# A four-layer graph network on one core: the attention passes' edge one-hots built on ScalarE, and the first pass's messages as four products with a per-partition scalar

## The chip, the cores and the metric

One NeuronCore of a Trainium2 chip runs the whole program. The metric is the time of one launch on the device, in microseconds (us). Engine names are those of the profile: PE (TensorE, matmuls), DVE (VectorE), ACT (ScalarE), POOL (GpSimd), SP (SyncE, which issues DMAs).

## What is computed

The input is a graph of 3,125 nodes with 128 features and 53,125 edges, sorted by target node. Four layers follow each other, each added to `x` after a layer norm with Relu. Cut to what matters:

```python
h = relu(layernorm(x)); x = x + gat(h)            # softmax over each target's edges, one head
h = relu(layernorm(x)); x = x + relational(h)     # sum of proj[src, type] into dst
h = relu(layernorm(x)); x = x + two_gcn_layers(h)
h = relu(layernorm(x)); x = x + two_transformer_convs(h)   # softmax attention, four heads

# an attention layer, for the edges e: src -> dst
alpha = score(q[dst], k[src]);  p = exp(alpha - segment_max(alpha, dst)[dst])
out   = segment_sum(v[src] * p, dst) / segment_sum(p, dst)
```

So there are three attention passes over the edges (the GAT layer, called the first pass, and the two transformer convolutions, called the second and third) and three linear passes (one relational, two GCN).

## The kernel before

**Tiles.** The 53,125 edges are padded to 13 chunks of 8 groups of 4 tiles of 128 edges: 104 groups, 416 tiles. One edge lies on one partition. Since edges are sorted by target, the targets of a tile lie in a window of 128 nodes, and those of a group in a span of 512.

**A pass of attention.** POOL issues for every tile one indirect DMA (line 465) that gathers the source rows of its 128 edges into a ring in SBUF (24 slots of one group in the first pass, 15 in the others); for a group beyond the ring it first waits for `msg_ready` of the group that had the slot. PE brings the target rows to the edges with a one-hot (node by edge) that ACT makes in `targets` (a Square, line 628, and a Relu, line 630). DVE makes the scores: in the second and third pass by a product for each group (`products`, which waits for the gather) and a reduction (`head_sums`), in the first pass once for each chunk (`scores`, which waits for all eight gathers of the chunk). A chain through DVE, PE and ACT once for each chunk gives the maxima and exponentials.

**The part that is changed.** DVE's `messages(s)` (line 880) does two things for group s, both as a tensor_tensor on 128 x 512 elements in float32 through the helper `tt` (line 716): the value rows times the factor of the edge (into `msg`, which signals `msg_ready`), and the one-hot by edge, `iota_j == dstP` with both inputs broadcast (into `Sb`, 3 slots, which signals `s_ready`). PE's `node_sums(s)` (line 1300) waits for `s_ready`, clears a PSUM bank `NU[s % 2]` and multiplies messages by one-hots into it, then does the same with the factors into `MTB`. DVE's `add_sums(s)` adds both to the sums in SBUF (`numS`, `extS`). DVE runs `messages(s - 11)` in its step s and `add_sums(s - 13)` before it in the same step, so `s_ready` and `msg_ready` of a group tell PE as well that the bank of two groups earlier has been read. PE runs `expand(s + 1)` and then `node_sums(s - 12)` in its step s.

**The order of ACT.** In each step s of its `attention` (line 618) ACT does `edge_terms(s)` (in the second and third pass it waits for DVE's product of group s and copies 16 columns, line 639), `targets(s + 4)`, and once in a chunk `exponentials(c)`, which waits for the maxima.

**A linear pass** gathers in the same way (line 479); DVE makes its one-hots with the same tensor_tensor, and has no messages to make.

## Time and profile before

| | us |
|---|---|
| median of three runs (3841.62, 3859.76, 3859.91) | 3859.76 |
| the profiled execution, its time | 3848.41 |
| the profiled execution, its span | 3846.6 |
| POOL busy in the span | 2596.3 (67%) |
| PE busy | 2344.7 (61%) |
| DVE busy | 1864.5 (48%) |
| ACT busy | 587.7 (15%) |
| mean granted TensorE clock | 0.706 |

Some 1.8 us lie around the span. How to read it: the busy shares are means over six passes with different limits. The gathers of the six passes run, by the span's clock, from 90 to 685 (first attention), 806 to 1327, 1387 to 1907 and 1943 to 2463 (linear), 2537 to 3104 and 3191 to 3768 us (second and third attention). Between and behind them lie stages without gathers: the end of an attention pass takes some 40 us after its last gather, and then tables are built. The page gives the chain of work that ended last, the groups of instructions, and the waits; a gap of 0.30 us before each gather is put down to "issue".

### The profile page before, as it was taken

Reading aid. Unit: us, or ns where it says so; the run is one execution under the profiler, and the core shown is the slowest. Engines: PE = TensorE matmul, PEld = TensorE weight load, DVE = VectorE, ACT = ScalarE, POOL = GpSimd, SP = SyncE. Lnnn points to the kernel's source line nnn. Section 1 sums busy time; section 2 is a strip of 40 time slices with the busy share of each in tenths; the row PEclk is TensorE's granted clock in tenths of the full one; section 3 lists DMA queues with packets and bytes.
Section 4 is the critical chain, followed back from the end, with each engine's and each line's share of the span. In section 5 each row is a group of like instructions: output and inputs, shape, how many; then the busy total and the mean of one; then the engine's idle time right before and its main releaser. Section 6 shows DMA issues by size and latency. Waiting matters only on the chain.

```text
span 3846.6 us, 42630 instructions
## 1 busy us (share of the span) xinstructions
PE 2344.7 (61%) x12256; PEld 1786.2 (46%) x12460; DVE 1864.5 (48%) x3957; ACT 587.7 (15%) x1289; POOL 2596.3 (67%) x2561
## 2 busy tenths in 40 slices
PE   4477777664444554444454444457777785777776
PEld 2465555333333343333333333336566654656665
DVE  4365555633322332222232222337777784777777
ACT  2322221220000020000000000132222202222220
POOL 1777777047777647777667777447777736777773
PEclk9988888865555565555555555568888896888888
DMA  4433333131222112212122221156666616656651
GB/s 93 87 73 74 73 72 63 66 110 53 53 53 53 43 47 53 53 53 53 45 58 53 53 53 53 41 167 171 167 170 176 170 57 184 170 164 167 169 162 36
DMA packets 345045, 356.63 MB, mean 93 GB/s; under 512 B 125614, under 2 KB 267637, under 8 KB 344821
## 3 DMA queue, kind: packets, MB, share of 16 engines
q0 software_dynamic: 93184, 219.12, 21.4%
q1 hardware_dynamic: 245494, 132.86, 13.1%
q10 hardware_dynamic: 6148, 1.93, 0.3%
q8 instruction: 114, 1.87, 0.2%
q14 instruction: 105, 0.86, 0.1%
HBM read 323.81 MB, written 30.05 MB: 92 GB/s over the span
## 4 chain that ended last, share of the span: by engine, by line
POOL 64%; issue 20%; PE 7%; DVE 4%; DMA 3%; ACT 1%; ACTq 1%; DVEq 0%; SPq 0%; POOLq 0%
POOL gathered_rows L465 33%; POOL gathered_rows L479 31%; PE QX L1157 4%; DMA gathered_rows<-key_value_rows,src_index 2%; PE NU L1157 1%; PE MTB L1157 1%; DVE messages L716 1%; ACTq L531 0%; DVE x_rows L716 0%; DVE query_key_products L716 0%; PE MID L1190 0%; DVE extra_sums_transposed L716 0%; PE MTB L1190 0%; ACT h_transposed L592 0%; DMA gcn_columns<-in_L_gnn_be_dram 0%
## 5 line engine op out<-in xcount | busy, mean ns | idle before, releaser
L1157 PE MATMUL NU<-gathered_rows 128*128 128x128 f32 x2496 | 636.8, 437 | 809.6 <-DMA gathered_rows<-gcn_rows,src_index 540.5
L465 POOL DMA_INDIRECT gathered_rows<-key_value_rows,src_index x832 | 889.1, 1069 | 312.0 <-issue 251.3
L479 POOL DMA_INDIRECT gathered_rows<-gcn_rows,src_index x832 | 785.8, 944 | 346.8 <-issue 252.9
L1157 PEld LDWEIGHTS NU<-gathered_rows 128*128 128x128 f32 x2496 | 554.5, 327 | 992.3 <-issue 977.1
L716 DVE TENSOR_TENSOR sums_transposed<-sums_transposed,NU 128x512 f32 x624 | 425.5, 682 | 1163.1 <-PE NU L1157 1160.4
L465 POOL DMA_INDIRECT gathered_rows<-gat_rows,src_index x416 | 467.8, 1125 | 207.5 <-issue 126.5
L479 POOL DMA_INDIRECT gathered_rows<-relation_rows,src_relation_index x416 | 393.9, 947 | 147.8 <-issue 126.5
L1157 PEld LDWEIGHTS NU<-edge_node_onehot,messages 128*128 128x128 f32 x2496 | 382.4, 219 | 17.7
L1157 PE MATMUL NU<-edge_node_onehot,messages 128*128 128x128 f32 x2496 | 379.0, 302 | 11.2 <-issue 3.0
L1157 PE MATMUL MTB<-edge_node_onehot,edge_factors 128*8 128x128 f32 (+1 forms) x2496 | 343.1, 283 | 0.0
L1157 PE MATMUL QX<-query_window,node_edge_onehot 128*128 128x132 f32 (+1 forms) x1248 | 201.6, 304 | 146.4 <-DMA query_window<-query_rows 81.1
L716 DVE TENSOR_TENSOR query_key_products<-QX,gathered_rows 128x512 f32<-128x512 f32 x208 | 142.1, 683 | 292.4 <-DMA gathered_rows<-key_value_rows,src_index 257.1
L628 ACT ACTIVATE window_distance<-dst_in_window_row,minus_partition 128x512 bf16<-128x512 bf16 x312 | 225.1, 721 | 336.9 <-PE QX L1157 279.1
L1157 PEld LDWEIGHTS MTB<-edge_node_onehot,edge_factors 128*8 128x8 f32 (+1 forms) x2496 | 232.8, 93 | 90.0 <-issue 11.2
L1157 PEld LDWEIGHTS QX<-query_window,node_edge_onehot 128*128 128x128 f32 x1248 | 176.4, 217 | 174.4 <-issue 161.2
L1157 PE MATMUL NU<-start_penalty,zero_weights 128*128 128x512 bf16 x420 | 239.5, 570 | 9.6 <-DVE edge_node_onehot L716 9.3
L716 DVE TENSOR_TENSOR extra_sums_transposed<-extra_sums_transposed,MTB 8x512 f32 (+1 forms) x312 | 209.3, 671 | 43.8 <-PE MTB L1157 43.4
L716 DVE TENSOR_TENSOR gathered_rows<-iota_window,dst_in_window_by_edge 128x512 f32<-128x512 f32 x312 | 212.6, 685 | 5.7 <-DMA relation_rows<-gathered_rows 5.7
L716 DVE TENSOR_TENSOR edge_node_onehot<-iota_window,dst_in_window_by_edge 128x512 f32<-128x512 f32 x312 | 211.2, 677 | 0.0
L716 DVE TENSOR_TENSOR messages<-gathered_rows,edge_factors 128x512 f32<-128x512 f32 x312 | 211.0, 676 | 0.0
L1157 PE MATMUL QX<-query_window,relation_weights 128*128 128x132 f32 x832 | 162.2, 356 | 77.3 <-DMA query_window<-query_rows 40.3
L1157 PEld LDWEIGHTS QX<-query_window,relation_weights 128*128 128x128 f32 x832 | 140.1, 252 | 100.1 <-issue 90.2
(255 smaller groups left out, 2206.7 us busy)
## 6 DMA issues: line engine op xcount, KB each, us to landing
query_window<-query_rows SPq DMA_DIRECT2D x832, 66.0 KB
dst_in_window_row<-dst_in_window SPq DMA_DIRECT2D x156, 256.0 KB, 3.5
gathered_rows<-gcn_rows,src_index POOLq DMA_INDIRECT x832, 2.5
gathered_rows<-key_value_rows,src_index POOLq DMA_INDIRECT x832
relation_rows<-gathered_rows SPq DMA_DIRECT2D x25, 512.0 KB, 2.6
gathered_rows<-gat_rows,src_index POOLq DMA_INDIRECT x416, 2.6
query_window<-gat_target_scores SPq DMA_DIRECT2D x416, 2.0 KB
gathered_rows<-relation_rows,src_relation_index POOLq DMA_INDIRECT x416, 2.5
```

What stands on the lines that cost most here:

```text
L465: pool.indirect_dma_start(out=rows_of(a, s)[:, t, :], out_offset=None, in_=a["table"], in_offset=bass.IndirectOffsetOnAxis(ap=srcI[:, TPG ...
L479: pool.indirect_dma_start(out=lrows[:, TPG * (K % LRING) + t, :], out_offset=None, in_=p["table"], in_offset=bass.IndirectOffsetOnAxis(ap= ...
L628: own.step(act.activation(STa[:, s % 2, :], drow_sb[:, half, q:q + TPG * P], ACT.Square, bias=neg_iota_p[:]))
L716: return dve.tensor_tensor(o, x, y, op)
L1157: return pe.matmul(o, l, r, start=start, stop=stop)
```

## The change

ACT takes over the one-hots by edge in all three attention passes. A new function `edge_onehots(s)` makes the four tiles of a group with four Square activations of 128 x 128 (`(dst - iota)^2`, the bias being the column of `dstP`), waits for its own last one, and turns them into ones and zeros with a Relu of `1 - x` over 128 x 512, in place. It is called at the end of ACT's step for group s - 10, two groups ahead of PE's use, and waits until PE has done with the slot, three groups earlier (`ex_ready`). ACT's loop runs 7 steps longer so that the last groups are covered. DVE no longer makes them. PE's `node_sums` waits for `msg_ready` as well as `s_ready`. In the first pass, which has one head, the messages of a group are no longer one tensor_tensor but four tensor_scalar products of 128 x 128 with the tile's factor as a per-partition scalar.

```diff
@@ scalar engine, attention
+                def edge_onehots(s):
+
+                    to = Sb[:, s % SBN]
+                    if s == 0 and k == 0:
+                        act.wait_ge(S["idx_ready"], 2)
+                    if s >= SBN:
+                        act.wait_ge(S["ex_ready"], b + s - SBN + 1)
+                    for t in range(TPG):
+                        last = act.activation(to[:, t, :], iota_j[:], ACT.Square,
+                                              bias=dstP[:, TPG * s + t:TPG * s + t + 1], scale=-1.0)
+                    own.step(last)
+                    act.wait_ge(own.sem, own.value())
+                    act.activation(to, to, ACT.Relu, bias=1.0, scale=-1.0).then_inc(S["s_ready"], 1)
+
                 for s in range(TS):
                     targets(s)
-                for s in range(NG + 3):
+                for s in range(NG + LAG - 2):
                     if s < NG:
                         edge_terms(s)
                     if s + TS < NG:
...
                     if r == 2 and 0 <= c < NCH:
                         exponentials(c)
+                    if 0 <= s + 2 - LAG < NG:
+                        edge_onehots(s + 2 - LAG)
@@ vector engine, messages(s)
-                    tt(msg[:, s % 2].rearrange("p t (h d) -> p t h d", h=H), v, f, ALU.mult).then_inc(S["msg_ready"], 1)
-                    tt(Sb[:, s % SBN], iota_j[:].unsqueeze(1).broadcast_to([P, TPG, P]),
-                       dstP[:, TPG * s:TPG * s + TPG].unsqueeze(2).broadcast_to([P, TPG, P]),
-                       ALU.is_equal).then_inc(S["s_ready"], 1)
+                    if L3:
+                        last = tt(msg[:, s % 2].rearrange("p t (h d) -> p t h d", h=H), v, f, ALU.mult)
+                    else:
+                        for t in range(TPG):
+                            last = dve.tensor_scalar(msg[:, s % 2, t, :], v[:, t, 0, :],
+                                                     pe8[:, s // GPC % 2, 0, TPG * g + t:TPG * g + t + 1], None, ALU.mult)
+                    last.then_inc(S["msg_ready"], 1)
@@ tensor engine, node_sums(s)
                     pe.wait_ge(S["s_ready"], sb0 + s + 1)
+                    pe.wait_ge(S["msg_ready"], b + s + 1)
                     clear(NU[s % 2], P)
```

## Rows read from the trace of the kernel before

**Rows 1.** The page's chain that ended last, by line.

```profile
POOL gathered_rows L465 33%; POOL gathered_rows L479 31%; PE QX L1157 4%; DMA gathered_rows<-key_value_rows,src_index 2%; PE NU L1157 1%; PE MTB L1157 1%; DVE messages L716 1%; ACTq L531 0%; DVE x_rows L716 0%; DVE query_key_products L716 0%; PE MID L1190 0%; DVE extra_sums_transposed L716 0%; PE MTB L1190 0%; ACT h_transposed L592 0%; DMA gcn_columns<-in_L_gnn_be_dram 0%
```

**Rows 2.** By stretch: length; busy PE, PEld, DVE, ACT, POOL; clock; DMA share, GB/s.

```profile
90.00:685.00 595.00, 405.70 (x2654) 321.62 (x2700) 310.24 (x689) 144.67 (x245) 467.82 (x416) 0.85 0.36 73
...
1387.00:1907.00 520.00, 252.30 (x922) 187.46 (x939) 137.65 (x214) 0.00 (x0) 393.12 (x416) 0.51 0.20 53
...
2537.00:3104.00 567.00, 406.87 (x2598) 332.54 (x2645) 403.58 (x813) 153.25 (x348) 439.56 (x416) 0.85 0.61 171
3104.00:3144.00 40.00, 33.87 (x248) 25.30 (x251) 36.51 (x74) 0.71 (x4) 0.00 (x0) 0.97 0.02 4
3191.00:3768.00 577.00, 413.22 (x2602) 333.87 (x2649) 403.99 (x813) 151.87 (x347) 449.55 (x416) 0.84 0.60 168
```

**Rows 3.** POOL's groups by form: busy, mean ns, idle before and releasers.

```profile
L479 POOL DMA_INDIRECT gathered_rows<-gcn_rows,src_index x832 | 785.8, 944 | 346.8 <-issue 252.9 <-DMA gcn_rows<-gathered_rows 93.9
L465 POOL DMA_INDIRECT gathered_rows<-gat_rows,src_index x416 | 467.8, 1125 | 207.5 <-issue 126.5 <-DMA gat_target_scores<-gathered_rows 81.1
```

**Rows 4.** Waits: POOL on messages, whole span; DVE on gathers, 2537 to 3104.

```profile
POOL gathered_rows L465 <- DVE messages L716: 7.6, 25, 0.3
...
DVE query_key_products L716 <- DMA gathered_rows<-key_value_rows,src_index: 122.8, 50, 4.7
```

**Rows 5.** Timeline of POOL and of DVE, 2616.8 to 2620, second attention pass.

```profile
2618.09 1.42 POOL L465 DMA_INDIRECT gathered_rows<-key_value_rows,src_index  x1 [0.30 <-issue]
...
2617.41 0.68 DVE L716 TENSOR_TENSOR messages<-gathered_rows,edge_factors 128x512 f32<-128x512 f32 x1
2618.01 0.69 DVE L716 TENSOR_TENSOR edge_node_onehot<-iota_window,dst_in_window_by_edge 128x512 f32<-128x512 f32 x1
```

**Rows 6.** Timeline of POOL and of DVE, 1100 to 1101.4, a linear pass.

```profile
1100.17 0.94 POOL L479 DMA_INDIRECT gathered_rows<-relation_rows,src_relation_index  x1 [0.30 <-issue]
...
1100.58 0.68 DVE L716 TENSOR_TENSOR gathered_rows<-iota_window,dst_in_window_by_edge 128x512 f32<-128x512 f32 x1
```

**Rows 7.** Timeline of the first pass: a burst, and DVE's wait ahead of a chunk.

```profile
437.75 1.73 POOL L465 DMA_INDIRECT gathered_rows<-gat_rows,src_index  x1 [0.30 <-issue]
...
436.78 0.68 DVE L716 TENSOR_TENSOR extra_sums_transposed<-extra_sums_transposed,MTB 3x512 f32 x1 [0.49 <-PE MTB L1157]
...
437.99 0.67 DVE L716 TENSOR_TENSOR edge_node_onehot<-iota_window,dst_in_window_by_edge 128x512 f32<-128x512 f32 x1
438.90 0.69 DVE L716 TENSOR_TENSOR sums_transposed<-sums_transposed,NU 128x512 f32 x1 [0.24 <-PE NU L1157]
440.08 0.68 DVE L716 TENSOR_TENSOR extra_sums_transposed<-extra_sums_transposed,MTB 3x512 f32 x1 [0.48 <-PE MTB L1157]
...
410.05 0.21 DVE L716 TENSOR_TENSOR query_edge_term<-gathered_rows,QX 128x32 f32<-128x32 f32 x1 [12.96 <-DMA gathered_rows<-gat_rows,src_index]
```

**Rows 8.** Timeline, 514.6 to 515.7: a gather and a small tensor_scalar that started in it.

```profile
514.65 0.95 POOL L465 DMA_INDIRECT gathered_rows<-gat_rows,src_index  x1 [0.30 <-issue]
...
515.18 0.46 DVE L946 TENSOR_SCALAR max_change_by_feature<-max_change,chunk_continues 1x128 f32<-1x128 f32 x1
```

**Rows 9.** Timeline at 31 us: eight tensor_scalar products of 128 x 128, no gather about.

```profile
31.12 1.65 DVE L742 TENSOR_SCALAR relation_weights<-query_key_products,relation_coefficients 128x128 f32<-128x128 f32 x8
```

**Rows 10.** ACT's groups by form: busy, mean ns, idle before and releasers.

```profile
L628 ACT ACTIVATE window_distance<-dst_in_window_row,minus_partition 128x512 bf16<-128x512 bf16 x312 | 225.1, 721 | 336.9 <-PE QX L1157 279.1 <-DMA dst_in_window_row<-dst_in_window 57.8
L630 ACT ACTIVATE node_edge_onehot<-window_distance 128x512 f32<-128x512 bf16 x156 | 98.2, 630 | 5.0
L586 ACT ACTIVATE normed_block<-x_rows,minus_mean_scaled,inverse_deviation 128x128 f32<-128x128 f32 x100 | 48.9, 492 | 14.7 <-DVE minus_mean_scaled L770 14.2 <-PE MTB L1190 0.2
L639 ACT COPY query_edge_term<-QX 128x16 f32<-128x16 f32 x208 | 38.8, 187 | 832.2 <-DVE query_key_products L716 825.6 <-PE QX L1157 6.5
...
L686 ACT ACTIVATE h_transposed<-sums_transposed,gcn_small 128x512 f32<-128x512 f32 x12 | 9.1, 802 | 1.4 <-DVE gcn_small L1107 1.4
```

**Rows 11.** Busy time in the end of the second pass, 3126 to 3141 (columns of Rows 2).

```profile
3126.00:3141.00 15.00, 14.24 (x110) 10.94 (x111) 15.00 (x26) 0.00 (x0) 0.00 (x0) 1.00 0.00 1
```

## The prediction

> **What bounds the kernel now.** I read the chain that ended last first, then busy time by stretch, then POOL's groups and waits, then the timeline of POOL beside that of DVE. The chain lies on POOL's gathers: 33% of the span at line 465 (attention), 31% at line 479 (linear) [rows 1]; before each gather lies a gap of 0.30 us [rows 5, 6]. Busy time by stretch says how much of each pass is POOL itself. A linear pass is 416 gathers, 393.1 us busy in 520: 0.945 us each, and with the gap 1.25 us, so 416 x 1.25 = 520 is the whole pass [rows 2, 3]. The attention passes have the same 416 gathers and the same gap (126.5 us for the first pass's 416 is 0.304 each), but are busy 467.8, 439.6 and 449.6 us [rows 2, 3]. The difference to 393.1 is 74.7, 46.5 and 56.5 us, 177.7 together, and it explains their 595, 567 and 577 us to a few tenths. So POOL never stands still in a pass; its gathers are stretched. It doesn't wait for its ring: the only wait on messages is 25 gaps of at most 0.3 us, no longer than the usual gap [rows 4]. DVE waits for gathers, not the reverse (122.8 us of the second pass) [rows 4]. **The prize is those 177.7 us**, plus what the ends of passes give.
>
> **What stretches a gather.** Lay the timelines side by side. In the second pass a gather starts at 2618.09, while DVE is in messages and one-hot, 2617.41 to 2618.70; it takes 1.42 us instead of 0.95 and ends at 2619.51, 0.82 after the one-hot's end [rows 5]. In the first pass a gather of 1.73 us (437.75 to 439.48) again ends 0.82 after the one-hot's end at 438.66 [rows 7]. So a gather that starts while DVE holds a pair of SBUF inputs waits for the end of the train and then needs 0.82 us; it loses what was left of the train less 0.12. In a linear pass a one-hot of 0.68 us that starts 0.41 us into the gather stretches nothing: 0.94 us [rows 6]. It has ended when the next gather begins; DVE's other two-input work there is of the same size, and the pass has no stretch at all [rows 2]. With the phase left to chance, a train of length T costs on average (T - 0.12)^2 / (2 x 1.25) for each group. For messages and one-hot, T = 2618.70 - 2617.41 = 1.29: 0.55 us, times 104 groups 57 us a pass; measured 74.7, 46.5, 56.5. The rule has the right size.
>
> **Part 1: the one-hots leave DVE in the second and third pass.** The train shrinks to the messages alone, 0.68 us [rows 5]: 0.56^2 / 2.5 = 0.125 us a group, 13 us a pass. Small two-input operations of the chunk's chain stay; for them I add 2 us and take 15 us of stretch a pass. Gain: 46.5 + 56.5 - 30 = **73 us**. Bounds: if the stretch only went down in proportion to the train (0.68/1.29 of 103 is 54) the gain is 49; if it vanished as in the linear passes, 103.
>
> **Part 2: what ACT takes.** For each group four Squares of 128 x 128 and a Relu of 128 x 512. No row shows that Square. From above: 0.49, the activation of the same size with two per-partition operands; from below, the 0.72 of the 512-column Square with one, less 384 columns at (0.80 - 0.49) / 384 us, the slope between the two sizes with two: 0.41 [rows 10]. The Relu goes by the 0.63 of line 630. So 2.2 to 2.6 us a group. With line 628, line 630 and the copy of line 639 (0.72 + 0.63 + 0.19) ACT's step is 3.8 to 4.2 us [rows 10] against the 5.0 us in which POOL now delivers a group at best. It is hidden, under POOL's gathers; by how much, 0.8 to 1.2 us. PE uses the one-hot two of its steps later, and ACT's wait for the slot is on PE work of three groups earlier, so both waits have a step or more in hand. Queued behind ACT's new wait are the next copy (for PE's expand), the next `targets` (four groups ahead) and once a chunk the exponentials, which DVE awaits; a delay of 2 us there falls within a chunk of 40 us in which DVE still waits for gathers. I cost it at nothing. PE's added wait for `msg_ready` is fulfilled 0.6 us earlier than the one-hot was: nothing. In the first pass's bursts PE and DVE do a group in 3.3 us (436.78 to 440.08) [rows 7]; ACT without the copy needs 3.6 to 4.0, which can make a burst of 8 up to 5 us longer, covered by the 13 us that DVE idles before each chunk [rows 7].
>
> **Part 3: the first pass's messages.** Eight tensor_scalar of this shape take 1.65 us [rows 9], with 0.28 for the last: 0.196 apart, so four make 3 x 0.196 + 0.28 = 0.87 us against 1.29 for the train before. If they only acted on a gather's start, the rule gives 0.75^2 / 2.5 = 0.225, 23 us for the pass. But a one-source operation meets the gather at its end too: the small tensor_scalar that starts at 515.18, 0.53 us into a gather, takes 0.46 instead of 0.27 and ends 0.04 after the gather does [rows 8]. If the four start in the last 0.45 us of a gather they are pushed to its end, run to 0.91 behind it, and the next gather, 0.30 behind, loses 0.91 - 0.30 + 0.82 - 0.945 = 0.48 us. Averaged over the phases that is 0.36 x 0.48 + 0.24 x 0.6 = 0.32 a group, 33 us. If, beyond that, they keep a gather in progress from finishing, another 0.4 us in 0.4 of the phases, 17 us, comes to it, 50. The first pass measures 1.3 times my rule (74.7 to 57), so from 23 to 62, I take 42. Gain: 74.7 - 42 = **33 us** (13 to 52). The Trainium skill has a rule for this, in "SBUF — State Buffer", section "Who interferes with whom": two SBUF inputs contend with GpSimd's reads, while tensor_scalar in its two-port mode shuts GpSimd out altogether, so that it can't write descriptors. The case of rows 8 points that way (they collide at the gather's end), and by that rule the first pass would keep its stretch.
>
> **Part 4: the ends.** After the last gather the second pass takes 40 us [rows 2]. In its middle both engines are full: PE 14.24 and DVE 15.00 of 15 us at full clock, 2.4 us a group [rows 11]. Taking 0.6 us off DVE doesn't help where PE needs the same 2.4. Only the chain of the last chunk, which DVE sets, gains: I take 1 us for each of three ends, **3 us**, between -3 (exponentials queued behind one-hots) and 7 (12 groups x 0.6) for each.
>
> **The sum.** 73 + 33 + 3 = 109 us off the profiled execution's 3848.4 (span 3846.6 and 1.8 around it): 3739. The median of the runs is 11 us above the profiled one, which would give 3751; I say 3745, between them.
>
> **Rivals.** *A: the products take back what they save in the first pass.* The push and the lockout together leave its stretch at 75 us: 3848 - 73 - 3 = 3772, 3784 by the median; 3778. For: rows 8. Against: the train is shorter by a third. It is also the time by the Trainium skill's rule above. *B: the passes aren't POOL's for long.* PE is busy 407 of 567 us in the second pass at a mean clock of 0.85 [rows 2], 3.9 us a group, and its chain waits come on top; with POOL at 5.05 us a group it may set the pace at 5.2, 0.15 x 208 = 31 us less gain: 3776. For: PE's share goes to 77% and more; against: DVE's 122.8 us of waiting for gathers would first have to be used up. *C: no stretch is left in passes 2 and 3*, as in the linear ones, and 23 in the first: 3853 - 103 - 52 - 3 = 3695. *D, slower: the four products take turns with gathers.* If each tensor_scalar is held to the end of a gather, as the one in rows 8, a group's messages take 4 x 1.25 = 5.0 us instead of 0.8. DVE's group is then 5.0 + 1.2 = 6.2, and a chunk 8 x 6.2 plus 7 for its chain (46 now, less 13 idle, less 8 x 3.3) = 57 us against 595 / 13 = 46 now; 11 x 13 chunks = 143 us, less 73: 70 slower, 3923. It decides from the point where a group's messages exceed about 3.5 us: the 1.2 of today, 0.7 idle in the burst (0.24 + 0.48) and 13/8 = 1.6 idle ahead of the chunk [rows 7]. Against: products queued back to back should go as a train, as messages and one-hot do now. *E: the change doesn't do what it says*, since ACT becomes the pace: it would need more than 5.0 us a group, and 5.7 to be slower than today, where I find at most 4.2; then 3850, no change.
>
> **Chances and range.** Forecast 0.64, A 0.13, B 0.10, C 0.05, D 0.04, E 0.04. The likeliest case alone spans 3845 less the gains' bounds, which are hardly all met at once: 3715 to 3780. The range of 8 in 10 takes in A, B and half of the way to C: 3702 to 3800. About 0.5% is what a measurement of this kernel can tell from no change, 19 us: faster 0.91, same 0.04, slower 0.05.
>
> **What would show it.** Right: gathers of line 465 at a mean near 0.98 us in passes 2 and 3 and 1.04 in the first, with the gap still 0.30; DVE busy down by some 190 us, ACT up by some 700 and still below 85% in any pass; no idle of PE before its sums put down to ACT. A shows as a first pass still at 1.1 us a gather; B as gaps above 0.30 before gathers, ended by messages; D as tensor_scalar products far above 0.28 us; E as PE's sums waiting for the one-hots. The prediction is wrong if POOL stands still for anything but its 0.30 us, or if single trains of 0.68 us hit gathers more often than by chance.

## The result, and the profile after

The changed kernel takes **3722.64 us**, the median of 4 runs (3713.34 to 3726.67), against 3856.38 for the kernel before (4 runs, 3841.62 to 3859.91): a ratio of 0.9658, 95% interval 0.9642 to 0.9674. The forecast was 3745, in a range of 3702 to 3800. The profiled execution took 3726.67 us (span 3724.8), 121.7 us less than the 3848.41 of before.

From the page of the changed kernel: busy time of each engine; the chain that ended last, by engine; the two groups of attention gathers; the two new groups on ScalarE (columns: busy us, mean ns | idle before and what ended it).

```profile
PE 2389.6 (64%) x12460; PEld 1788.2 (48%) x12460; DVE 1711.9 (46%) x3957; ACT 1147.3 (31%) x2849; POOL 2460.8 (66%) x2561
...
POOL 57%; issue 19%; PE 13%; DVE 5%; DMA 3%; ACT 1%; ACTq 1%; SPq 1%; DVEq 0%; POOLq 0%
...
L465 POOL DMA_INDIRECT gathered_rows<-key_value_rows,src_index x832 | 816.6, 982 | 318.3 <-issue 252.8
...
L465 POOL DMA_INDIRECT gathered_rows<-gat_rows,src_index x416 | 403.9, 971 | 209.4 <-issue 124.7
...
L659 ACT ACTIVATE edge_node_onehot<-iota_window,dst_in_window_by_edge 128x128 f32<-128x128 f32 x1248 | 394.6, 386 | 27.3 <-PE MTB L1176 25.1
...
L663 ACT ACTIVATE edge_node_onehot<-edge_node_onehot 128x512 f32<-128x512 f32 x312 | 196.5, 630 | 9.9
```

The chain still lies on POOL. From here on, **stretch** is the busy time of a pass's 416 gathers less the 393.1 us that they take in an undisturbed linear pass [rows 2]. It is read off the two groups: 403.9 - 393.1 = 10.8 us in the first pass (before 74.7 [rows 3]), and 816.6 - 786.2 = 30.4 in the second and third together (before 46.5 + 56.5 = 103). Line 465's share of the chain is 25%, before 33% [rows 1].

By stretch of time, the three attention passes of the changed kernel (length; busy PE, PEld, DVE, ACT, POOL; clock; DMA share, GB/s):

```profile
92.00:623.00 531.00, 423.88 (x2700) 329.75 (x2700) 277.22 (x875) 315.86 (x725) 403.93 (x416) 0.86 0.41 82
2483.00:3018.00 535.00, 403.89 (x2650) 325.92 (x2651) 351.80 (x720) 319.74 (x813) 407.79 (x416) 0.86 0.66 181
...
3110.00:3645.00 535.00, 403.96 (x2650) 326.91 (x2651) 351.62 (x720) 318.65 (x812) 408.40 (x416) 0.86 0.66 181
```

They answer to 595, 567 and 577 us [rows 2]: 64, 32 and 42 less. That is the stretch and nothing else: 531 is 416 gathers of 0.971 us and their gaps of 0.305. What lies outside the passes gained nothing: the stages between them and the tail add up to 565 us in this profile, 551 before, and 550 in a second profile of the changed kernel, so the 14 us more of this one are most likely scatter between executions and not a cost of the change.

The messages on VectorE, from its groups by form, and two moments of the first pass, POOL beside VectorE (start, duration):

```profile
L732 DVE TENSOR_TENSOR messages<-gathered_rows,edge_factors 128x512 f32<-128x512 f32 x208 | 140.9, 677 | 0.0
L904 DVE TENSOR_SCALAR messages<-gathered_rows,edge_factors 128x128 f32<-128x128 f32 x416 | 95.5, 291 | 0.0
```

```profile
244.47 1.07 DVE L904 TENSOR_SCALAR messages<-gathered_rows,edge_factors 128x128 f32<-128x128 f32 x4
244.56 0.94 POOL L465 DMA_INDIRECT gathered_rows<-gat_rows,src_index  x1 [0.30 <-issue]
...
277.32 1.29 POOL L465 DMA_INDIRECT gathered_rows<-gat_rows,src_index  x1 [0.30 <-issue]
277.63 1.01 DVE L904 TENSOR_SCALAR messages<-gathered_rows,edge_factors 128x128 f32<-128x128 f32 x4
278.91 0.94 POOL L465 DMA_INDIRECT gathered_rows<-gat_rows,src_index  x1 [0.30 <-issue]
```

At 244.5 a gather starts 0.09 us into the four products and takes its plain 0.94; it is the products that pay, 1.07 us against 0.86 where no gather runs beside them. At 277.3 the products begin 0.31 us after the gather and it takes 1.29. Over the first pass, the 54 gathers that start in the 0.6 us after the first product's start lose 0.05 us on average, the 34 that start in the 0.6 us ahead of it 0.18 (each by its own length less 0.945).

### The profile page after: what moved, and what is told of

Its sections match the earlier page's. It is cut to its first block, busy times and chain, and to the rows that moved or that the text cites. A ratio compares the mean times of both kernels' runs of the same rounds, so it can differ in the third digit from the quotient of the medians.

```text
span 3724.8 us, 44708 instructions
## 1 busy us (share of the span) xinstructions
PE 2389.6 (64%) x12460; PEld 1788.2 (48%) x12460; DVE 1711.9 (46%) x3957; ACT 1147.3 (31%) x2849; POOL 2460.8 (66%) x2561
## 4 chain that ended last, share of the span: by engine, by line
POOL 57%; issue 19%; PE 13%; DVE 5%; DMA 3%; ACT 1%; ACTq 1%; SPq 1%; DVEq 0%; POOLq 0%
POOL gathered_rows L479 32%; POOL gathered_rows L465 25%; PE QX L1176 6%; PE NU L1176 3%; PE MTB L1176 3%; DMA gathered_rows<-key_value_rows,src_index 2%; DVE messages L732 1%; ACTq L531 1%; DMA query_window<-gat_target_scores 0%; PE MID L1176 0%; DMA open_tiles<-end_ahead_penalty 0%; DVE query_key_products L732 0%; DVE x_rows L732 0%; PE MID L1209 0%; PE MTB L1209 0%
## 5 line engine op out<-in xcount | busy, mean ns | idle before, releaser
L465 POOL DMA_INDIRECT gathered_rows<-key_value_rows,src_index x832 | 816.6, 982 | 318.3 <-issue 252.8
L465 POOL DMA_INDIRECT gathered_rows<-gat_rows,src_index x416 | 403.9, 971 | 209.4 <-issue 124.7
L659 ACT ACTIVATE edge_node_onehot<-iota_window,dst_in_window_by_edge 128x128 f32<-128x128 f32 x1248 | 394.6, 386 | 27.3 <-PE MTB L1176 25.1
L1176 PE MATMUL MTB<-edge_node_onehot,edge_factors 128*8 128x128 f32 (+1 forms) x2496 | 358.7, 292 | 0.0
L1176 PE MATMUL NU<-start_penalty,zero_weights 128*128 128x512 bf16 x624 | 329.5, 528 | 10.4 <-DVE messages L732 9.9
L663 ACT ACTIVATE edge_node_onehot<-edge_node_onehot 128x512 f32<-128x512 f32 x312 | 196.5, 630 | 9.9
```

The lines of the kernel that those rows point to most:

```text
L465: pool.indirect_dma_start(out=rows_of(a, s)[:, t, :], out_offset=None, in_=a["table"], in_offset=bass.IndirectOffsetOnAxis(ap=srcI[:, TPG ...
L659: last = act.activation(to[:, t, :], iota_j[:], ACT.Square, bias=dstP[:, TPG * s + t:TPG * s + t + 1], scale=-1.0)
L663: act.activation(to, to, ACT.Relu, bias=1.0, scale=-1.0).then_inc(S["s_ready"], 1)
L1176: return pe.matmul(o, l, r, start=start, stop=stop)
```

## Experiments

My theory going in was that of the prediction: VectorE's operations with two SBUF inputs hold a gather that starts among them, and what is gained is the shorter train of such work. The rivals: the length of VectorE's chain or of its instructions counts, not their inputs; short instructions let a gather in between; the products with a per-partition scalar, not the one-hots, bring the gain; ScalarE has no room. Every edit is against the changed kernel, unless it says otherwise. The first four kernels ran on another chip than all the rest and are told last. A gather's **loss** is its own length less 0.945 us.

### The changed kernel again

> The changed kernel once more, beside the kernel before on the same chip. In the first group of runs the kernel before itself took 4493 us, 16% more than the 3856 it took where the change was measured, and its linear passes took 588 us and not 520, with gaps of 2 to 8 us before gathers; so this run says which of the two conditions holds here. My theory: where linear passes take 520 us, the ratio is 0.966 as before, with 11, 15 and 16 us of stretch over 0.945 us a gather in the three attention passes. Rival (the gaps of the first group are a property of that chip and hit every kernel alike): linear passes of 588 us, the same small stretch, but a ratio within 0.5% of 1.01, because gaps and not the stretch set the passes there.

3716.98 us (3707.84 to 3722.22) beside 3850.09 for the kernel before: 0.9655 (0.9627 to 0.9684). Stretch 11.4, 12.0 and 19.0 us, linear passes 520 us. This is the base for the next three.

### One-hots alone

```diff
-                    if L3:
-                        last = tt(msg[:, s % 2].rearrange("p t (h d) -> p t h d", h=H), v, f, ALU.mult)
-                    else:
-                        for t in range(TPG):
-                            last = dve.tensor_scalar(...)
+                    last = tt(msg[:, s % 2].rearrange("p t (h d) -> p t h d", h=H), v, f, ALU.mult)
```

> One-hots on ScalarE in all three attention passes, the first pass's messages as one product over the group as before the change. In the first group of runs this kernel's stretch was 17, 19 and 17 us. My theory (a train of 0.68 us of two-input work costs a gather little, the pair of messages and one-hot much): the same 15 to 20 us in each pass, so the one-hots bring nearly all of the gain also in the first pass, and where linear passes take 520 us the time is within 10 us of the changed kernel: ratio 0.966 to 0.969. Rival (the four products are what saved the first pass): its stretch stays at 40 or more and the time is 25 us or more above the changed kernel, ratio 0.973 or more.

3744.18 us (3739.89 to 3762.29), ratio 0.9737 (0.9699 to 0.9774), 27 us above the changed kernel. Its two groups of gathers, and a moment of its first pass:

```profile
L465 POOL DMA_INDIRECT gathered_rows<-key_value_rows,src_index x832 | 824.6, 991 | 311.1 <-issue 254.3
...
L465 POOL DMA_INDIRECT gathered_rows<-gat_rows,src_index x416 | 432.4, 1039 | 207.0 <-issue 126.4
```

```profile
260.45 0.68 DVE L732 TENSOR_TENSOR extra_sums_transposed<-extra_sums_transposed,MTB 3x512 f32 x1 [0.49 <-PE MTB L1171]
260.82 1.73 POOL L465 DMA_INDIRECT gathered_rows<-gat_rows,src_index  x1 [0.30 <-issue]
261.06 0.67 DVE L732 TENSOR_TENSOR messages<-gathered_rows,edge_factors 128x512 f32<-128x512 f32 x1
```

My expectation fell, and the rival's numbers came in. The second and third pass are as in the changed kernel (38.4 us together), but the first keeps 432.4 - 393.1 = 39.3 us. So **both parts count in the first pass**: the one-hots take it from 74.7 to 39.3, the products from 39.3 to 11. The moment shows why one two-input message of 0.67 us costs more there than I had it: the gather had started 0.24 us *before* the messages, and is held all the same, to 0.82 us after their end (261.73 + 0.82 = 262.55). Most starts up to 0.45 us ahead are caught in this pass; 29 gathers that began 0.15 to 0.45 us ahead of the messages lost 0.73 on average.

Of the pass's 39.3 us, 27 are lost by gathers that start in the 0.6 us ahead of the messages, and 9 by those that start during them. Widening the prediction's rule by 0.45 us gives (0.56 + 0.45)^2 / 2.5 = 0.41 us a group, 42 us a pass, near the 39.3; but for the train of before it gives 109 where 74.7 were measured, so it is no rule either. In the second pass 20 gathers in the same position lost only 0.16. What VectorE does just before the messages goes with it: in eight profiles in which linear passes take 520 us, of the gathers that start 0.15 to 0.45 us ahead of two-input work, all 60 lost more than 0.4 us where `extra_sums_transposed` came before that work, none of 78 where `max_after_tile` did, and 68 of 258 where `query_key_products` did. Why is not shown.

### The one-hots stay on VectorE, cut in four, one input each (edit of the kernel before)

```diff
-                    tt(Sb[:, s % SBN], iota_j[:].unsqueeze(1).broadcast_to([P, TPG, P]),
-                       dstP[:, TPG * s:TPG * s + TPG].unsqueeze(2).broadcast_to([P, TPG, P]),
-                       ALU.is_equal).then_inc(S["s_ready"], 1)
+                    for t in range(TPG):
+                        last = dve.tensor_scalar(Sb[:, s % SBN, t, :], iota_j[:], dstP[:, TPG * s + t:TPG * s + t + 1], None, ALU.is_equal)
+                    last.then_inc(S["s_ready"], 1)
```

> The kernel before with only this edit: the one-hot by edge stays on VectorE in all three attention passes but is made by four tensor_scalar of 128 x 128 (is_equal with a per-partition scalar) and not by one operation with two SBUF inputs over 128 x 512. Messages stay as they were. My theory (short instructions hand the port over between them, so that a gather gets in after at most one of them): the train is as long as before, 0.68 + 4 x 0.2, but the stretch falls from 75, 46 and 56 us to 20 to 35 in each pass; the time falls by 75 to 110 us, ratio 0.971 to 0.981, without any work moved to ScalarE. Rival 1 (length of the train is what counts, whatever it is cut into): stretch as in the kernel before, ratio 0.99 to 1.00. Rival 2 (the two-port mode of tensor_scalar shuts GpSimd out for the whole train): stretch above the kernel before, ratio above 1.00.

3772.91 us (3763.96 to 3778.35), ratio 0.9796 (0.9769 to 0.9822).

```profile
L465 POOL DMA_INDIRECT gathered_rows<-key_value_rows,src_index x832 | 833.7, 1002 | 311.2 <-issue 253.0
...
L465 POOL DMA_INDIRECT gathered_rows<-gat_rows,src_index x416 | 439.6, 1057 | 207.9 <-issue 125.9
...
L886 DVE TENSOR_SCALAR edge_node_onehot<-iota_window,dst_in_window_by_edge 128x128 f32<-128x128 f32 x1248 | 283.9, 284 | 0.0
```

The train of messages and one-hots is longer than before the change, 1.49 us against 1.27, yet the stretch is 46.5 us in the first pass and 47.5 in the other two together, 7 and 9 more than with the one-hots on ScalarE. The time and the two later passes came in as expected (22.7 and 24.7 us); the first pass's 46.5 lies above my 20 to 35. Both rivals fall. **Most of what moving the one-hots to ScalarE brings is to be had on VectorE**, by giving them one SBUF input: 84 of 100 us of stretch (178 to 94, against 178 to 78), and 77 of 106 us of time. This doesn't say yet whether it is the single input or the shortness of the four.

### The messages of passes two and three cut in four, two inputs as before

```diff
-                        last = tt(msg[:, s % 2].rearrange("p t (h d) -> p t h d", h=H), v, f, ALU.mult)
+                        for t in range(TPG):
+                            last = tt(msg[:, s % 2, t, :].rearrange("p (h d) -> p h d", h=H), v[:, t], f[:, t], ALU.mult)
```

> The changed kernel, and in the second and third pass the messages too are made by four operations of 128 x 128, with two SBUF inputs as they were. My theory (it is the length of one instruction that a gather waits out): the 15 and 16 us of stretch fall to 3 to 10 each, and the time is 8 to 20 us under the changed kernel, ratio to it 0.995 to 0.998. Rival (two-input instructions back to back hold on as one train, now 0.8 us long): 20 to 25 us of stretch each, 8 to 15 us slower than the changed kernel.

3711.68 us (3706.09 to 3713.57), ratio 0.9638 (0.9617 to 0.9659): 5 us under the changed kernel, which the two intervals don't tell apart. Gathers of the two passes, and two moments of the second:

```profile
L465 POOL DMA_INDIRECT gathered_rows<-key_value_rows,src_index x832 | 814.7, 979 | 311.1 <-issue 255.7
```

```profile
2608.55 1.72 POOL L465 DMA_INDIRECT gathered_rows<-key_value_rows,src_index  x1 [0.30 <-issue]
2608.56 0.88 DVE L732 TENSOR_TENSOR messages<-gathered_rows,edge_factors 128x128 f32<-128x128 f32 x4
...
2627.47 0.99 POOL L465 DMA_INDIRECT gathered_rows<-key_value_rows,src_index  x1 [0.30 <-issue]
2627.36 0.88 DVE L732 TENSOR_TENSOR messages<-gathered_rows,edge_factors 128x128 f32<-128x128 f32 x4
```

814.7 - 786.2 = 28.5 us of stretch against 31.1 in the run beside it. Neither my 6 to 20 nor the rival's 40 to 50. The moments show that both happen. The first gather isn't let in between the four: it ends 0.83 us after the last of them (2609.44), just as with one long operation. The second starts 0.11 us into the four and is let in: it ends 0.22 us after the last of them, which is 0.82 after the first.

Of the 94 gathers that start early enough in the four to be held to their end, 56 were, 27 ended 0.82 us after the first, second or third, and 11 lost nothing; of the 79 that start so in the single operation of the run beside it, 78 were held to its end. The four together last 0.88 us and not 0.67, for which the rule asks 34 us from those 94; being let in halves it to 17.5, so the sum stays where it was (20.8 in the run beside it). **Shortness helps some gathers, but with two inputs it gained nothing that can be told from scatter**, so it is not what brought the 84 us of the run before. What decides whether a gather is let in isn't shown.

### One more VectorE operation for each group: one input, then two

To settle inputs against length, two kernels add behind each group's messages an operation whose result nobody uses. In both it waits for its own predecessor (left out here), and is written here with `spare` for the unused tile.

```diff
                     last.then_inc(S["msg_ready"], 1)
...
+                    dve.tensor_reduce(spare, iota_j[:].unsqueeze(1).broadcast_to([P, TPG, P]), AX.X, ALU.add)...
```

> The changed kernel, and behind each group's messages VectorE makes one more operation whose result nobody uses: a tensor_reduce of 128 x 512 with ONE SBUF input. Each of its instructions is as long as a two-input product. On the other chip this kernel's stretch stayed at 6 to 9 us a pass. My theory (only the second SBUF input holds a gather's reads, the length of an instruction doesn't matter): the stretch stays at 10 to 20 us in each of the three attention passes. VectorE gets 0.67 us more for a group, some 70 us a pass, beside gathers that still set the pace; only the ends of passes and the chunk's chain pay: 0 to 25 us over the changed kernel in all. Rival (any long VectorE instruction between a gather's start and its reads holds it): 30 us or more of stretch a pass, as for messages and one-hot before the change, 60 to 120 us over the changed kernel.

```profile
L466 POOL DMA_INDIRECT gathered_rows<-key_value_rows,src_index x832 | 816.8, 982 | 313.9 <-issue 254.8
...
L466 POOL DMA_INDIRECT gathered_rows<-gat_rows,src_index x416 | 403.3, 969 | 206.5 <-issue 124.0
...
L912 DVE TENSOR_REDUCE normed_block<-iota_window 128x4 f32<-128x512 f32 x312 | 209.3, 671 | 0.0
```

3723.41 us (3717.82 to 3729.78), ratio 0.9672 (0.9643 to 0.97): 312 operations of 671 ns cost nothing that can be measured, and the stretch is that of the changed kernel to a few tenths (10.2 and 30.6 us).

```diff
                     last.then_inc(S["msg_ready"], 1)
...
+                    tt(spare, iota_j[:].unsqueeze(1).broadcast_to([P, TPG, P]),
+                       dstP[:, TPG * s:TPG * s + TPG].unsqueeze(2).broadcast_to([P, TPG, P]), ALU.is_equal)...
```

> The changed kernel, and behind each group's messages VectorE makes again the comparison with TWO SBUF inputs that the change took away (same operands, result to a spare tile, nobody waits for it). Nothing else goes back: ScalarE still makes the one-hots in use. My theory: the stretch comes back, 40 to 65 us in passes two and three, 30 to 60 in the first (its four products are one-input, so the train there is shorter than before the change), together 110 to 170 of the 178 before; time 70 to 125 us over the changed kernel. Rival (the gain came from a shorter VectorE chain, or from who produces the one-hots, not from the port): the same as with the added reduction, whose instructions are as long.

```profile
L466 POOL DMA_INDIRECT gathered_rows<-key_value_rows,src_index x832 | 893.9, 1074 | 311.0 <-issue 251.1
...
L466 POOL DMA_INDIRECT gathered_rows<-gat_rows,src_index x416 | 446.7, 1074 | 208.2 <-issue 124.7
...
L734 DVE TENSOR_TENSOR normed_block<-iota_window,dst_in_window_by_edge 128x512 bf16<-128x512 f32 x312 | 211.3, 677 | 0.0
```

3834.91 us (10 runs, 3826.13 to 3847.92), ratio 0.9961 (0.9943 to 0.998). As many operations, 677 ns against 671, and the stretch is 53.6 + 107.7 = 161 us, of the 178 before the change. ScalarE still makes the one-hots in use; **the comparison costs 111 us more than the reduction of the same length** (3834.91 less 3723.41), more than 80% of the change's gain. This pair of runs carries the explanation.

The two operations differ in one more thing than their inputs: the comparison writes 512 columns, the reduction 4. The changed kernel's own trace settles that. VectorE's additions of the node sums write 512 columns and are as long, but one of their two inputs, `NU`, lies in PSUM:

```profile
L732 DVE TENSOR_TENSOR sums_transposed<-sums_transposed,NU 128x512 f32 x624 | 426.6, 684 | 1237.2 <-PE NU L1176 1236.2
```

In its three attention passes 140 gathers start during one of them with no messages about; the average loss is 0.00 us, the largest 0.01. So neither length nor the columns written hold a gather; a second input in SBUF does.

### No message with two SBUF inputs at all

```diff
                     if L3:
-                        last = tt(msg[:, s % 2].rearrange("p t (h d) -> p t h d", h=H), v, f, ALU.mult)
+                        for t in range(TPG):
+                            for h in range(H):
+                                last = dve.tensor_scalar(msg[:, s % 2, t, HD * h:HD * h + HD], v[:, t, h, :],
+                                                         pe8[:, s // GPC % 2, h, TPG * g + t:TPG * g + t + 1], None, ALU.mult)
```

> The changed kernel, and in the second and third pass the messages are sixteen tensor_scalar of 128 x 32 for a group (one for each tile and head, factor per partition), so that no product of messages has two SBUF inputs in any pass. My theory (two SBUF inputs are what a gather waits for; four short two-input products saved nothing, 28.5 us of stretch against 31): 12 to 19 us of stretch in passes two and three fall to 3 to 8 each. VectorE pays for it: sixteen at 0.07 to 0.13 us against 0.68, 0.4 to 1.4 us more a group, free within a pass as long as its group stays below 5.0 us, paid at the three ends of passes with 12 groups each: time -15 to +25 us against the changed kernel. Rival (it is a train of VectorE instructions on the port that counts, one input or two): the train is now 1.2 to 2 us long and the stretch goes up to 40 us or more in each of the two passes.

```profile
L465 POOL DMA_INDIRECT gathered_rows<-key_value_rows,src_index x832 | 791.8, 952 | 374.1 <-issue 230.1
...
L903 DVE TENSOR_SCALAR messages<-gathered_rows,edge_factors 128x32 f32<-128x32 f32 x3328 | 518.4, 246 | 0.0
```

Its second pass (timeline), its waits of POOL (us in total, times, longest), and the pass by stretch:

```profile
2603.61 2.68 DVE L903 TENSOR_SCALAR messages<-gathered_rows,edge_factors 128x32 f32<-128x32 f32 x16
2604.07 0.95 POOL L465 DMA_INDIRECT gathered_rows<-key_value_rows,src_index  x1 [0.30 <-issue]
...
POOL gathered_rows L465 <- DVE messages L903: 84.8, 94, 3.0
...
2476.00:3027.00 551.00, 392.90 (x2595) 311.60 (x2596) 496.18 (x2058) 316.70 (x801) 395.73 (x416) 0.88 0.63 176
```

3786.65 us (3785.7 to 3789.95), ratio 0.9836 (0.9811 to 0.9861). The theory of the two inputs holds at its sharpest: a train of 2.68 us leaves the gather in it at 0.95, and the two passes' stretch falls to 791.8 - 786.2 = 5.6 us. But **the price was mis-sized**, and the time is 70 us above the changed kernel where I expected -15 to +25: a product of a quarter of the columns takes 246 ns against 291, so sixteen take 518.4 / 208 = 2.49 us a group and not 1.1 to 2.1. VectorE is busy 496 of 551 us, and gathers now wait for it. These waits for messages are 28 us a pass over the usual gaps, and the stretches of time behind the two passes grow by 20 us each (110 and 101 us against 90 and 80). 25 us of stretch gained, some 95 lost.

### How much cover ScalarE has

```diff
+                    for again in range(2):
+                        for t in range(TPG):
+                            last = act.activation(spare[:, t, :], iota_j[:], ACT.Square,
+                                                  bias=dstP[:, TPG * s + t:TPG * s + t + 1], scale=-1.0)
+                        ...
                     for t in range(TPG):
                         last = act.activation(to[:, t, :], iota_j[:], ACT.Square,
```

> The changed kernel, and before each group's four Squares ScalarE makes eight more of the same kind into a spare tile (2 x 1.28 us a group). My theory (ScalarE's step of 3.1 to 3.5 us is hidden under the 5.0 us in which GpSimd delivers a group, with 1.5 to 1.9 us of cover): 5.7 to 6.1 us a group exceed the cover, gathers get gaps ended by messages, and each attention pass lasts 590 to 635 us instead of 533; in all 170 to 300 us over the changed kernel. Rival (VectorE and PE wait for ScalarE anyway, so there is no cover now): all 2.56 x 104 = 266 us a pass are paid, some 800 us over it.

By stretch: the first pass and the stage behind it, the second pass, and the stage behind that.

```profile
91.00:628.00 537.00, 412.00 (x2363) 318.18 (x2364) 244.91 (x777) 465.98 (x1273) 403.23 (x416) 0.82 0.39 79
628.00:827.00 199.00, 149.72 (x737) 90.86 (x735) 97.44 (x339) 150.60 (x391) 3.37 (x2) 0.90 0.19 72
2559.00:3130.00 571.00, 386.19 (x2586) 313.49 (x2586) 347.08 (x711) 523.78 (x1514) 419.67 (x416) 0.89 0.62 170
3130.00:3244.00 114.00, 84.29 (x475) 57.60 (x475) 69.85 (x176) 67.42 (x216) 20.78 (x17) 0.90 0.15 46
```

3924.49 us (3919.05 to 3931.14), ratio 1.02 (1.0171 to 1.0229), 207 us over the changed kernel. That is within the 170 to 300 expected, but not where I put it: I expected 590 to 635 us for each pass, and they last 536, 570 and 570. The first pass lasts only 5 us longer, since its ring of 24 groups lets the gathers run on while ScalarE falls behind; the bill comes after it, 199 us instead of 121. Pass and stage together cost 83, 63 and 55 us more, 0.8, 0.6 and 0.5 us for each of 104 groups. The eight Squares add 2.48 us a group in the trace (from the first Square to the end of the Relu, 4.40 us against 1.92), so 1.7 to 1.95 us of it were covered. That is the room which the change's own one-hots left, if anything too small a figure: the gathers of the second and third pass are also stretched more here, 54.8 us against 31.0, which is 24 of the 207 us.

### The same four questions on another chip

The first four kernels ran on a chip where the kernel before itself took 4492.87 us (19 runs, 4464.72 to 4507.96).

> The one-hots by edge on ACT in all three attention passes, but the first pass's messages left as one tensor_tensor of 128 x 512. Port theory (a gather is stretched by what is left of one two-input DVE instruction, and can slip in between short ones): passes 2 and 3 as in the changed kernel, stretch 14 to 16 us each; in the first pass a single instruction of 0.68 us instead of four of 0.27, stretch 13 to 20 us instead of 10.8; time 3725 to 3735, a little above the changed kernel's 3722. Rival (what counts is DVE's time): DVE has 0.2 us less for each group of the first pass, so 3705 to 3722, below it.

> The kernel before with only the first pass's messages as four tensor_scalar products; all one-hots stay on DVE. Port theory: gathers slip in between the products and only the one-hot's 0.68 us stays as a block, so the first pass's stretch falls from 74.7 us to 25 to 40, passes 2 and 3 keep their 103: 3805 to 3825. Rival (DVE's time): DVE has 0.2 us more for each group of the first pass, nothing is gained: 3856 to 3870. If the products shut POOL out as a block of 0.87 us that grows the train to 1.5 us: first pass slower by 10 to 25 us, 3865 to 3880.

> The changed kernel with a reduction of 128 x 512 to 128 x 4 added on DVE behind the messages of every group, about 0.67 us with one SBUF input: DVE is as busy as before the change, but with nothing that takes two SBUF inputs. Its result isn't used. Port theory: time as the changed kernel, 3715 to 3732, stretch unchanged. Rival (DVE's time): back to the kernel before, 3840 to 3860.

> The changed kernel with the old compare of 128 x 512 with two SBUF inputs added on DVE behind the messages of every group, into a scratch tile in bf16 that nobody reads: the DVE train of before, while ACT still makes the one-hots that are used. Port theory: passes 2 and 3 get their 103 us of stretch back (from 30), the first pass some 15 to 30 us: 3805 to 3830. Rival (DVE's time): the same as with the added reduction. If both cost nothing, the gain came from PE's earlier start, not from DVE at all: 3722.

Measured there: one-hots alone 4546.7 us, ratio 1.0116 (1.0092 to 1.014); products alone (the kernel before with the change's four tensor_scalar) 4495.96, 1.0013 (0.9997 to 1.0028); added reduction 4607.19, 1.0255 (1.0231 to 1.0279); added comparison 4507.65, 1.0032 (1.0007 to 1.0057). One-hots alone, its page (gathers) and a linear pass by stretch; then the gathers of products alone:

```profile
L465 POOL DMA_INDIRECT gathered_rows<-key_value_rows,src_index x832 | 822.0, 988 | 693.6 <-DVE messages L732 378.9
...
L465 POOL DMA_INDIRECT gathered_rows<-gat_rows,src_index x416 | 410.5, 987 | 379.9 <-DVE messages L732 177.1
...
1622.00:2210.00 588.00, 182.51 (x878) 160.56 (x893) 130.07 (x204) 0.00 (x0) 401.47 (x416) 0.57 0.18 47
```

```profile
L465 POOL DMA_INDIRECT gathered_rows<-key_value_rows,src_index x832 | 927.9, 1115 | 554.8 <-issue 252.7
...
L465 POOL DMA_INDIRECT gathered_rows<-gat_rows,src_index x416 | 426.5, 1025 | 342.9 <-DVE messages L888 141.0
```

The stretch goes as on the other chip: over the three passes 53 us with one-hots alone, 22 with the added reduction, 190 with the added comparison, 175 with the products alone. But it no longer sets the time. Even a linear pass, which none of these kernels touches, takes 588 us and not 520, with some 18 gaps of 0.4 to 8 us between its gathers; in the attention passes such gaps add 108 to 213 us each, and most there are ended by messages. The two kernels with little stretch were the slower ones there: their gaps over the three attention passes sum to 552 us (one-hots alone) and 619 (added reduction), against 373 (products alone) and 365 (added comparison), 180 us and more for 120 to 170 of stretch. So of these four expectations no time held, and the stretches only in part: the first pass with the products alone (33 us of 25 to 40) and with one-hots alone (17) came in, and the two kernels with two-input one-hots or comparisons had 142 and 155 us in the second and third pass, not 103. The changed kernel itself wasn't run there; whether it wins or loses on such a chip is open. So is the cause of the gaps: with one-hots alone the profile puts 1471.5 us of VectorE's waits for sums down to no instruction at all, up to 23.9 us at a time, where on the usual chip the same waits are PE's and last at most 5.3.

## Why the prediction came out right, step by step

**The bound and the prize** were right. POOL's gathers set the passes before and after, the gap stayed at 0.305 us with none longer inside a pass, and each pass shrank by what its stretch did, to within a microsecond.

**The rule for the stretch** had the right size by two errors that offset each other. It counts the gathers that start in a train, and makes 57 us a pass for 104 groups. In the trace of before only 92 groups' trains run beside gathers, and the gathers that start in them lost 40, 36 and 41 us in the three passes: of the rest, 32, 8 and 14 were lost by gathers that start up to 0.6 us ahead of a train, which the rule leaves out. Nor is each held to the train's end: in the second and third pass of before, 35 of 161 ended 0.82 us after the messages, though the one-hot followed at once. And in the first pass the phase is not left to chance: 38 of the 67 gathers that start in a train start 0.3 to 0.45 us into it, and lost 0.80 us each.

**Part 1**, the one-hots in the second and third pass: 30 us of stretch forecast, 30.4 measured (31.1 in the second profile), a gain of 72.6 against 73. That it fits to a microsecond is in part luck: by the trace 17 of the 30 were lost by gathers that start in the messages, where the rule has 26, and 12 by those that start ahead of them, where I had put 4 for small operations. The added comparison, which gives 111 us back, confirms the cause, two SBUF inputs, and the added reduction and the additions of the node sums exclude the length.

**Part 2**, ScalarE's share: the Squares take 386 ns and not 410 to 490, ScalarE is busy 320 of 535 us, 3.1 a group against my 3.8 to 4.2, and its cover is 1.7 to 1.95 us, not 0.8 to 1.2. Costed at nothing, rightly. PE's added wait for messages ended some 10 us of idle time in the whole span.

**Part 3 is the term that was mis-sized.** I forecast 42 us left in the first pass; 10.8 are. The gain is 63.9 and not 33, outside the 13 to 52 that I gave it (and 50 times 1.3 is 65, not the 62 behind that 13). Two steps were wrong, and only the first enters the 42. First, the price of a one-input train: I let the four products act on a gather's start like two-input work (23 us) and pushed the next gather besides (17 more). The runs show 0.05 us for a gather that starts within them; they take turns, and the products pay. The row on which I built the second term, a small tensor_scalar that ended with its gather [rows 8], was read rightly for the tensor_scalar and wrongly for the gather behind it. Second, my rule only counted gathers that start after the train has begun; in the first pass most of those up to 0.45 us ahead are caught too, so a two-input message alone costs 39 us there and not 13. The single factor of 1.3 with which I scaled the rule to the first pass hid this.

The gather amid the products at 244.56 took 0.94 us, the one amid sixteen of them at 2604.07 took 0.95, and the stretch fell in both kernels. The Trainium skill, "SBUF — State Buffer", section "Who interferes with whom", says that a VectorE instruction in a two-port mode and GpSimd exclude each other for a whole instruction, whichever issued first having the ports. I had used it as a lock that always falls on the gather, and so kept the first pass's stretch (rival A, 3778). The runs show neither: the two take turns at each short product, and it is mostly the product that waits. Whether these tensor_scalar run in that mode at all, and whether a long one would hold a gather for its whole length, no run here shows. What the page says of two SBUF inputs, that such an instruction contends with a GpSimd one that reads SBUF, the runs bear out (161 us of stretch with the added comparison, 41 with the added reduction).

**Part 4**, the ends: 3 us forecast, none seen. The three stretches behind the attention passes were 121.7, 88.0 and 79.1 us before and 121.0, 89.7 and 80.1 in the second profile of the changed kernel; VectorE's relief there is lost in PE's equal need [rows 11].

**The sum**: 73 + 33 + 3 = 109 forecast; 72.6 + 63.9 - 14 (the scatter between the passes) = 122 measured in the profiled pair. By medians it is 133.7, since the profiled execution of before lay 8 us under its median and that of after 4 above. So the scatter hid about half of what Part 3 missed in the profiled pair; against the medians the forecast gain is 25 us short.

**The rivals.** A would have shown a first pass at 1.1 us a gather; it was 0.971. B would have shown gaps ended by messages; there were none above 0.32 us. It comes true when VectorE is loaded by 1.8 us a group more, as with sixteen products. C wanted none left in the second and third pass, where 30.4 us stayed, and 23 in the first, where 10.8 did: it failed where it differed from my forecast, though its first pass was nearer. D needed products far above 0.28 us; they took 0.291. E needed ScalarE above 5.0 us a group, and appears at some 5.6, with eight more Squares. Of the signs named beforehand, three were off: VectorE's busy time fell by 153 us and not 190, ScalarE's rose by 560 and not 700, and the first pass's gathers took 0.971 us and not 1.04.

## What to carry to other kernels

Where GpSimd's gathers set the pace, look at each VectorE operation beside them for its number of SBUF inputs, not for its length: a one-input operation of 0.67 us for each group cost nothing here, a two-input one 111 us. This holds where the gathers follow each other without gaps; on the other chip, where they didn't, the kernels with the least stretch were the slower ones. An operation whose second input is the same along the free axis can become tensor_scalar with a per-partition operand and stay on VectorE; most of the gain is there without a second engine (77 of 106 us of time), as long as the pieces don't get small (128 x 32 took 0.25 us, 128 x 128 0.29). No tensor_scalar longer than those ran beside gathers here. And a rule calibrated on one moment of a trace should be laid over all gathers of a pass, by their start against the train's start, before it is used for another length.

## What the runs showed of the hardware that I had not expected

- Gathers and short tensor_scalar take turns, mostly at the latter's cost: a product of 128 x 128 alone takes some 0.27 us, one that meets a gather up to 0.52.
- A gather that starts during one two-input operation ends 0.82 or 0.83 us after it (78 of 79). With four back to back in 0.88 us, 56 of 94 waited for the fourth, 27 only for an earlier one, and 11 for none.
- Two-input work that begins after a gather's start can still catch it, in the first pass up to 0.45 us later (0.73 us lost on average), in the second seldom (0.16). In the linear passes, where some 80 of 104 one-hots begin 0.3 to 0.5 us into a gather, there is no stretch to speak of (at most 0.7 us a pass in the kernel before).
- A Square of 128 x 128 with a per-partition bias takes 386 ns, and four back to back 1.26 us.
- The same kernel took 3850 us on one chip and 4493 on another, with TensorE's mean granted clock at 0.70 on both; 0.67 us of VectorE's work a group that was free on the first (ratio 0.967 with it, 0.966 without) went with a ratio of 1.026 on the second.
